# Softmax row sums inverted by GpSimd with a power of -1 in place of VectorE's reciprocal, in an attention block with an fp8 linear layer

## The chip, the cores and the metric

The kernel runs on one core of one Trainium2 chip. The metric is the device time of one execution in microseconds. Engine names in the rows: PE is TensorE, PEld its weight loads, DVE is VectorE, ACT is ScalarE, POOL is GpSimd, SP is SyncE, whose queue issues all the transfers.

## The reference, cut to what matters

The input x has the shape (8, 2048, 512). It is layer-normalised, then goes through an attention whose sequence axis is the first one (length n = 8), so that each of the 2048 columns is a batch entry with 16 heads of width 32, and through a linear layer with fp8 operands. The outputs and x are added.

```python
xn = _layernorm(x)
qkv = xn @ Wqkv.T + bqkv                    # n = 8, b = 2048, 16 heads of 32
mask = _prompt_mask(n, 4, 7, x.dtype)       # rows 0 to 3 see keys 0 to 3, rows 4 to 7 see all 8
scores = mask + scale * jnp.einsum('bnd,bmd->bnm', q, k)
attn = jax.nn.softmax(scores, axis=-1)      # the row sums of this softmax are what is inverted
out = jnp.einsum('bnm,bmd->bnd', attn, v)   # then @ Wproj.T + bproj
x = x + attention(xn) + fp8_linear(xn)
```

## The kernel before

The work is cut into 128 tiles of 128 rows (one sequence position, 128 batch entries). Eight consecutive tiles are the eight positions of the same 128 batch entries and make a group; there are 16 groups. Because of the mask, the first four tiles of a group see 4 keys ("light") and the last four see 8 ("heavy"). With so few keys, scores and the weighted sum of values are made by elementwise products and reductions and not by TensorE: one unit is 2048 products per partition. A light tile has one unit on each side, a heavy tile has two.

The kernel is one software pipeline. Every engine runs the same list of slots (`run_slots`), one slot for each tile, and does in slot j the stage with lag L for tile n = j - L. The lags that matter here: VectorE's statistics 1, the power that makes `rstd` 2, x's split into two fp16 parts 3, scores (L_QK) 8, exponential and row sum (L_SOFT) 9, probabilities and products with the values (L_PV) 11, the sum over these products (L_SUM) 12, its split 13, output projection and residual sum (L_PROJ) 15. Engines are in order and synchronise by counting semaphores: a wait holds everything that is behind it on the same engine. The order inside a slot is written by hand:

- VectorE: `bn_stats` (L722), `o_nat` sums of one or two units (L731), `bn_aggr` (L736), product and reduction of the first unit of scores (L694, L698), `row_sum` (L745), reciprocal (L748), the second unit of scores if there is one, row maximum (L758), its subtraction (L761).
- ScalarE: the exponential (L473) is first in the slot and waits for that subtraction; behind it lie, among others, both halves of the normalisation, the splits and `projected` (L516).
- GpSimd: `probs` (L399), the first unit of `prod_pv` (L388), the residual sum into `xs` (L407, waits for `projected`), the split of `o` (L412), `rstd` as a power of -0.5 on one column (L418), the split of `x` (L423), and, for a heavy tile, the second unit of `prod_pv` (L388).

`exps` and `inv_sum` have rings of four tiles, `probs` of two, `prod_pv` of four units. `row_sum` has one buffer. The slots overlap so that scores are heavy in four slots of eight and the products with the values in another four.

Of the kernel before, what the change touches and what calls it, by code (L numbers as in the profile page):

```python
# [5 lines left out]
F32 = mybir.dt.float32  # L6
# [4 lines left out]
ALU = mybir.AluOpType  # L11
ACT = mybir.ActivationFunctionType
AX_X = mybir.AxisListType.X

P = 128
# [3 lines left out]
H = 16  # L19
# [25 lines left out]
def keys_of(n):  # L45
    return PROMPT if n % N < PROMPT else N
# [17 lines left out]
def tile_count(i, n):  # L64
    return i * PAIR + (n + 1)
# [11 lines left out]
def after(eng, sem, count):  # L77
    if not isinstance(count, int) or count > 0:
        eng.wait_ge(sem, count)  # L79
# [20 lines left out]
def attention_and_fp8_linear(nc, x, Wqkv, bqkv, Wproj, bproj, Wffn, bffn, out):  # L100
# [3 lines left out]
    with ExitStack() as ctx:  # L104
        def sb(name, shape, dt):
            return ctx.enter_context(nc.sbuf_tensor(name, shape, dt))
# [25 lines left out]
        out_scale = sb("out_scale", [P, 1], F32)  # L132
        out_unscale = sb("out_unscale", [P, 1], F32)
        minus_half = sb("minus_half", [P, 1], F32)

        xn = sb("xn", [P, 4, C], F32)
# [18 lines left out]
        scores = sb("scores", [P, H, N], F32)  # L156
        shifted = sb("shifted", [P, H, N], F32)
        exps = sb("exps", [P, 4, H, N], F32)
        row_sum = sb("row_sum", [P, H], F32)
        inv_sum = sb("inv_sum", [P, 4, H], F32)  # L160
        probs = sb("probs", [P, 2, H, N], F32)
        prod_pv = sb("prod_pv", [P, PRODS, QUAD], F32)
        o_nat = sb("o_nat", [P, 2, C], F32)
# [32 lines left out]
        consts_set = sem("consts_set")  # L196
# [139 lines left out]
        @block.gpsimd  # L336
        def _(pool):
            nc.gpsimd.memset(ident[:, :], 0.0).then_inc(consts_set, 1)
            pool.wait_ge(consts_set, 1)
            nc.gpsimd.affine_select(out=ident[:, :], in_=ident[:, :], compare_op=ALU.not_equal, fill=1.0,  # L340
                                    base=0, pattern=[[-1, P]], channel_multiplier=1).then_inc(ident_ready, 1)
            nc.gpsimd.memset(ones[:, :], 1.0).then_inc(consts_set, 1)
            nc.gpsimd.memset(minus_half[:, :], -0.5).then_inc(consts_set, 1)
            nc.gpsimd.memset(out_bias_rows[:, :], 0.0).then_inc(consts_set, 1)

            pool.wait_ge(amax_parts, 1)
            nc.gpsimd.partition_all_reduce(amax[:, 6:8], amax[:, 4:6], P,
                                           bass.bass_isa.ReduceOp.max).then_inc(amax_ready, 1)

            def split_into_rows(b, rows):  # L350

                hi, mid, low = bias_parts
                nc.gpsimd.tensor_copy(hi, b).then_inc(bias_steps, 1)
                pool.wait_ge(bias_steps, 2)
                nc.gpsimd.tensor_tensor(bias_rest, b, hi, ALU.subtract).then_inc(bias_steps, 1)
                pool.wait_ge(bias_steps, 3)
                nc.gpsimd.tensor_copy(mid, bias_rest).then_inc(bias_steps, 1)
                pool.wait_ge(bias_steps, 4)
                nc.gpsimd.tensor_tensor(bias_rest, bias_rest, mid, ALU.subtract).then_inc(bias_steps, 1)
                pool.wait_ge(bias_steps, 5)  # L360
                nc.gpsimd.tensor_copy(low, bias_rest).then_inc(bias_steps, 1)
                pool.wait_ge(bias_steps, 6)
                pool.wait_ge(consts_set, 4)
                for k, part in enumerate((hi, mid, low)):
                    nc.gpsimd.tensor_copy(rows[32 * k:32 * k + 1, :], part[32 * k:32 * k + 1, :]).then_inc(bias_rows_ready, 1)
                    pool.wait_ge(bias_rows_ready, k + 1)

            pool.wait_ge(scales_ready, 1)
            pool.wait_ge(bk_loaded, 16)
            nc.gpsimd.tensor_scalar(k_bias[:, :], k_bias[:, :], scale[:, 0:1], 1.0, ALU.mult, ALU.mult).then_inc(k_bias_ready, 1)  # L370
            pool.wait_ge(bq_loaded, 16)
            nc.gpsimd.tensor_scalar(q_bias[:, :], q_bias[:, :], scale[:, 0:1], 1.0, ALU.mult, ALU.mult).then_inc(q_bias_ready, 1)
            pool.wait_ge(out_biases_loaded, 32)
            nc.gpsimd.tensor_tensor(bo_all, bo_all, bffn_all, ALU.add).then_inc(bias_steps, 1)
            pool.wait_ge(bias_steps, 1)
            nc.gpsimd.tensor_scalar(bo_all, bo_all, out_unscale[:, 0:1], 1.0, ALU.mult,
                                    ALU.mult).then_inc(out_biases_scaled, 1)

            def products(i, n, unit):
                u, h, heads = unit  # L380
                keys = keys_of(n)
                v = v_all[:, (n // N) % 2, h * D:(h + heads) * D, 0:keys].rearrange("p (h d) m -> p h d m", d=D)
                p = probs[:, n % 2, h:h + heads, 0:keys].unsqueeze(2).broadcast_to([P, heads, D, keys])
                o = prod_pv[:, u % PRODS, :].rearrange("p (h d m) -> p h d m", d=D, m=keys)
                after(pool, probs_ready, tile_count(i, n))
                after(pool, v_kept, tile_count(i, N * (n // N) + keys - 1))
                after(pool, pv_summed, unit_count(i, u - PRODS))
                nc.gpsimd.tensor_tensor(o, v, p, ALU.mult).then_inc(pv_multiplied, 1)  # L388

            def slot(i, j):  # L390
                if at(i, j, L_SOFT):
                    pool.wait_ge(out_bias_summed, 1)
                    split_into_rows(bo_all, out_bias_rows)
                if live(i, j, L_PV):
                    n = j - L_PV
                    keys = keys_of(n)
                    after(pool, inv_ready, tile_count(i, n))
                    after(pool, pv_multiplied, unit_count(i, last_unit(n - 2)))
                    nc.gpsimd.tensor_tensor(probs[:, n % 2, :, 0:keys], exps[:, n % 4, :, 0:keys],  # L399
                                            inv_sum[:, n % 4, :].unsqueeze(2).broadcast_to([P, H, keys]),  # L400
                                            ALU.mult).then_inc(probs_ready, 1)
                    products(i, n, head_units(n)[0])
                if live(i, j, L_PROJ):
                    n = j - L_PROJ
                    after(pool, proj_scaled, tile_count(i, n))
                    after(pool, res_loaded[n % 4], 16 * ring_count(i, n, 4))
                    nc.gpsimd.tensor_tensor(xs[:, n % 4, :], xs[:, n % 4, :], projected[:, :],  # L407
                                            ALU.add).then_inc(y_ready, 1)
                if live(i, j, L_SPLIT):
                    n = j - L_SPLIT  # L410
                    after(pool, o_hi_ready, tile_count(i, n))
                    nc.gpsimd.tensor_tensor(o16[:, n % 2, C:2 * C], o_nat[:, n % 2, :], o16[:, n % 2, 0:C],  # L412
                                            ALU.subtract).then_inc(o_lo_ready, 1)
                if live(i, j, L_CENTRE):
                    n = j - L_CENTRE
                    after(pool, var_ready, tile_count(i, n))
                    after(pool, xn_ready, tile_count(i, n - 2))
                    nc.gpsimd.tensor_tensor(rstd[:, n % 2, :], var_eps[:, :], minus_half[:, :],  # L418
                                            ALU.pow).then_inc(rstd_ready, 1)
                if live(i, j, L_NORM):  # L420
                    n = j - L_NORM
                    after(pool, x_hi_q_ready, tile_count(i, n))
                    nc.gpsimd.tensor_tensor(x16[:, n % 2, C:2 * C], xn[:, n % 4, :], x16[:, n % 2, 0:C],  # L423
                                            ALU.subtract).then_inc(x_lo_ready, 1)
                if live(i, j, L_PV):
                    n = j - L_PV
                    for unit in head_units(n)[1:]:
                        products(i, n, unit)

            run_slots(pool, slot)  # L430
# [206 lines left out]
        def _(dve):  # L637
# [64 lines left out]
            def slot(i, j):  # L702
# [37 lines left out]
                if live(i, j, L_SOFT):  # L740
                    n = j - L_SOFT
                    keys = keys_of(n)
                    after(dve, exps_ready, tile_count(i, n))
                    after(dve, inv_ready, tile_count(i, n - 1))
                    nc.vector.tensor_reduce(row_sum[:, :], exps[:, n % 4, :, 0:keys], AX_X, ALU.add).then_inc(sum_ready, 1)  # L745
                    after(dve, sum_ready, tile_count(i, n))
                    after(dve, probs_ready, tile_count(i, n - 4))
                    nc.vector.reciprocal(inv_sum[:, n % 4, :], row_sum[:, :]).then_inc(inv_ready, 1)  # L748
                if live(i, j, L_QK):
                    n = j - L_QK  # L750
                    keys = keys_of(n)
# [35 lines left out]
```

## Time and profile before

| | |
|---|---|
| median of 3 runs | 1708.37 us (1707.04 to 1708.56) |
| profiled execution, its own time | 1709.81 us |
| its span, first to last instruction | 1707.7 us |
| outside the span | 2.1 us |
| mean granted TensorE clock | 0.978 of full speed |
| busy shares | PE 89%, DVE 89%, POOL 80%, ACT 60% |

The span is that of one execution. Busy durations of neighbouring instructions of one engine overlap by some hundredths of a microsecond, so what an instruction takes from its engine is read from start to start rather than from its duration.

### The profile page before, as it was taken

How to read it: one execution, taken by the hardware profiler on the slowest of the kernel's cores; microseconds unless marked ns; L12 is line 12 of the kernel's file. 1: busy time of each engine (PE TensorE's matmuls, PEld its weight loads, DVE VectorE, ACT ScalarE, POOL GpSimd, SP SyncE). 2: the span in 40 equal slices, each digit the busy share in tenths (PEclk: the TensorE clock that was granted, in tenths of full speed). 3: DMA queues.
4: the chain of work that ended last, by engine and by line, in shares of the span. 5: the costliest groups of instructions: out<-in, count | busy, mean ns of one | idle time of the engine just before them, and what ended most of it. 6: DMA issues, size and time to landing. Idle time of an engine off the chain costs nothing.

```text
span 1707.7 us, 24850 instructions
## 1 busy us (share of the span) xinstructions
PE 1517.0 (89%) x6791; PEld 677.6 (40%) x6913; DVE 1518.7 (89%) x1380; ACT 1025.5 (60%) x1946; POOL 1373.5 (80%) x854
## 2 busy tenths in 40 slices
PE   4998898989989998998989899898998989899855
PEld 3443343434434443443434344343443434344312
DVE  6499898989989999999989899898998899999892
ACT  5665666656656666556566666666666666666422
POOL 2368879697896979879697887969788796978877
PEclk8999999999999999999999999999999999999978
DMA  5343534445354354444444444444444444453332
GB/s 188 72 99 90 123 99 109 117 99 130 98 124 105 97 130 98 117 112 111 109 105 113 106 116 105 114 111 101 119 105 119 105 105 116 104 124 85 90 71 77
DMA packets 366532, 184.30 MB, mean 108 GB/s; under 512 B 314160, under 2 KB 314160, under 8 KB 366384
## 3 DMA queue, kind: packets, MB, share of 16 engines
q1 hardware_dynamic: 366384, 182.53, 43.9%
q8 instruction: 68, 1.11, 0.3%
q14 instruction: 80, 0.66, 0.2%
HBM read 73.41 MB, written 33.55 MB: 63 GB/s over the span
## 4 chain that ended last, share of the span: by engine, by line
POOL 35%; issue 30%; DVE 26%; PE 4%; ACT 3%; POOLq 1%; DVEq 1%; DMA 0%; ACTq 0%; SPq 0%
POOL prod_pv L388 22%; DVE prod_qk L694 14%; DVE scores L698 6%; POOL o L412 4%; POOL x L423 4%; POOL xs L407 3%; POOL rstd L418 2%; DVE stats L722 2%; PE k_ps L579 1%; PE v_ps L579 1%; POOL probs L399 1%; DVE q_ps L758 1%; DVE row_sum L745 1%; PE q_ps L579 1%; POOLq L79 1%
## 5 line engine op out<-in xcount | busy, mean ns | idle before, releaser
L388 POOL TENSOR_TENSOR prod_pv<-kv,probs 128x2048 f32<-128x2048 f32 x192 | 813.0, 4234 | 16.2 <-POOL probs L399 11.1
L731 DVE TENSOR_REDUCE o_nat<-prod_pv 128x256 f32<-128x2048 f32 (+1 forms) x192 | 436.1, 2284 | 92.3 <-POOL prod_pv L388 72.5
L698 DVE TENSOR_REDUCE scores<-prod_qk 128x64 f32<-128x2048 f32 x192 | 439.4, 2288 | 7.3
L579 PE MATMUL k_ps<-wqkv_hi,xT 128*128 128x512 f16 x1024 | 334.1, 388 | 118.2 <-DMA xT<-x 118.1
L694 DVE TENSOR_TENSOR prod_qk<-q_ps,kv 128x2048 f32<-128x2048 f32 x192 | 432.0, 2250 | 2.5 <-ACT kv L534 2.5
L407 POOL TENSOR_TENSOR xs<-xs,projected 128x512 f32<-128x512 f32 x128 | 162.4, 1269 | 238.5 <-ACT projected L516 237.9
L579 PE MATMUL proj_ps<-wproj_hi,oT 128*128 128x512 f16 x1032 | 336.4, 388 | 6.3 <-ACT proj_ps L527 6.3
L579 PE MATMUL v_ps<-wqkv_hi,xT 128*128 128x512 f16 x1024 | 326.0, 380 | 0.0
L579 PE MATMUL q_ps<-wqkv_hi,xT 128*128 128x512 f16 x1024 | 325.4, 379 | 0.0
L473 ACT ACTIVATE exps<-shifted,exp_scale 128x64 f32<-128x64 f32 (+1 forms) x128 | 47.8, 373 | 365.8 <-DVE shifted L761 365.6
L579 PEld LDWEIGHTS k_ps<-wqkv_hi,xT 128*128 128x128 f16 x1024 | 101.8, 99 | 272.7 <-issue 144.8
L543 ACT ACTIVATE kv<-v_ps 128x512 f32<-128x512 f32 x128 | 141.3, 1104 | 113.9 <-PE v_ps L579 113.8
L579 PE MATMUL proj_ps<-wproj_lo,oT 128*128 128x512 f16 x516 | 201.1, 390 | 0.0
L579 PE MATMUL k_ps<-wqkv_lo,xT 128*128 128x512 f16 x512 | 198.9, 388 | 0.0
L579 PE MATMUL v_ps<-wqkv_lo,xT 128*128 128x512 f16 x512 | 194.5, 380 | 0.0
L579 PE MATMUL q_ps<-wqkv_lo,xT 128*128 128x512 f16 x512 | 194.0, 379 | 0.0
L423 POOL TENSOR_TENSOR x<-xn,x 128x512 f16<-128x512 f32 x128 | 148.3, 1159 | 17.4 <-ACT x L510 17.4
L534 ACT ACTIVATE kv<-k_ps 128x512 f32<-128x512 f32 x128 | 75.4, 589 | 133.1 <-PE k_ps L579 133.1
L412 POOL TENSOR_TENSOR o<-o_nat,o 128x512 f16<-128x512 f32 x128 | 148.3, 1159 | 5.6 <-ACT o L491 5.6
L579 PEld LDWEIGHTS proj_ps<-wproj_hi,oT 128*128 128x128 f16 x1032 | 102.7, 100 | 125.4 <-issue 9.8
L579 PEld LDWEIGHTS v_ps<-wqkv_hi,xT 128*128 128x128 f16 x1024 | 100.5, 98 | 121.8 <-issue 1.7
L579 PEld LDWEIGHTS q_ps<-wqkv_hi,xT 128*128 128x128 f16 x1024 | 100.2, 98 | 120.8
(115 smaller groups left out, 1727.9 us busy)
## 6 DMA issues: line engine op xcount, KB each, us to landing
xn<-in_L_attn_x SPq DMA_DIRECT2D x128, 256.0 KB, 2.8
xs<-in_L_attn_x SPq DMA_DIRECT2D x128, 256.0 KB, 2.9
out<-xs SPq DMA_DIRECT2D x128, 256.0 KB, 2.0
xT<-x SPq DMA_TRANSPOSE x256, 3.0
kv<-in_L_attn_Wqkv SPq DMA_DIRECT2D x3, 1024.0 KB, 10.6
oT<-o SPq DMA_TRANSPOSE x128, 3.2
kv<-in_L_ffn_weight SPq DMA_DIRECT2D x1, 1024.0 KB, 5.6
kv<-in_L_attn_Wproj SPq DMA_DIRECT2D x1, 1024.0 KB, 14.6
```

The costliest lines, as they stand in the source:

```text
L388: nc.gpsimd.tensor_tensor(o, v, p, ALU.mult).then_inc(pv_multiplied, 1)
L407: nc.gpsimd.tensor_tensor(xs[:, n % 4, :], xs[:, n % 4, :], projected[:, :], ALU.add).then_inc(y_ready, 1)
L412: nc.gpsimd.tensor_tensor(o16[:, n % 2, C:2 * C], o_nat[:, n % 2, :], o16[:, n % 2, 0:C], ALU.subtract).then_inc(o_lo_ready, 1)
L418: nc.gpsimd.tensor_tensor(rstd[:, n % 2, :], var_eps[:, :], minus_half[:, :], ALU.pow).then_inc(rstd_ready, 1)
L423: nc.gpsimd.tensor_tensor(x16[:, n % 2, C:2 * C], xn[:, n % 4, :], x16[:, n % 2, 0:C], ALU.subtract).then_inc(x_lo_ready, 1)
L473: nc.scalar.activation(exps[:, n % 4, :, 0:keys], shifted[:, :, 0:keys], ACT.Exp, scale=exp_scale[:, 0:1]).then_inc(exps_ready, 1)
L534: nc.scalar.activation(k_all[:, g % 2, n % N, :], k_ps[:, :], ACT.Copy).then_inc(k_kept, 1)
L543: nc.scalar.activation(v_all[:, g % 2, :, n % N], v_ps[:, :], ACT.Copy).then_inc(v_kept, 1)
L579: last = nc.tensor.matmul(acc[:, :], t[:, tc, :], w[:, c, col:col + 512], start=first and k == 0, stop=k == len(parts) - 1, skip_group_che ...
L694: nc.vector.tensor_tensor(prod_qk[:, :].rearrange("p (m c) -> p m c", c=C), qb, k, ALU.mult).then_inc(qk_multiplied, 1)
L698: nc.vector.tensor_reduce(scores[:, :, m0:m0 + 4].rearrange("p h m -> p m h"), prod_qk[:, :].rearrange("p (m h d) -> p m h d", h=H, d=D), ...
L731: nc.vector.tensor_reduce(o_nat[:, n % 2, h * D:(h + heads) * D], prod_pv[:, u % PRODS, :].rearrange("p (c m) -> p c m", m=keys), AX_X, AL ...
```

## The change

GpSimd makes the inverse of the row sums itself, with `pow` and an exponent of -1, in the same slot and directly in front of the probabilities that use it. VectorE's reciprocal is gone. So `row_sum` gets a ring of four tiles (it has to live from VectorE's slot n + 9 to GpSimd's slot n + 11), `inv_sum` gets one buffer, and the waits follow: VectorE waits for the probabilities of tile n - 4 ahead of the row sum and no longer for `inv_ready` and `sum_ready`; GpSimd waits for `sum_ready` of tile n and `probs_ready` of tile n - 1 ahead of the power, and for its own `inv_ready` ahead of the probabilities. A constant column of -1 is set once at the start.

```diff
+        minus_one = sb("minus_one", [P, 1], F32)
...
-        row_sum = sb("row_sum", [P, H], F32)
-        inv_sum = sb("inv_sum", [P, 4, H], F32)
+        row_sum = sb("row_sum", [P, 4, H], F32)
+        inv_sum = sb("inv_sum", [P, H], F32)
...
+            nc.gpsimd.memset(minus_one[:, :], -1.0).then_inc(consts_set, 1)
...
-                pool.wait_ge(consts_set, 4)
+                pool.wait_ge(consts_set, 5)
...
+                    after(pool, sum_ready, tile_count(i, n))
+                    after(pool, probs_ready, tile_count(i, n - 1))
+                    nc.gpsimd.tensor_tensor(inv_sum[:, :], row_sum[:, n % 4, :],
+                                            minus_one[:, :].broadcast_to([P, H]), ALU.pow).then_inc(inv_ready, 1)
                     after(pool, inv_ready, tile_count(i, n))
                     after(pool, pv_multiplied, unit_count(i, last_unit(n - 2)))
                     nc.gpsimd.tensor_tensor(probs[:, n % 2, :, 0:keys], exps[:, n % 4, :, 0:keys],
-                                            inv_sum[:, n % 4, :].unsqueeze(2).broadcast_to([P, H, keys]),
+                                            inv_sum[:, :].unsqueeze(2).broadcast_to([P, H, keys]),
                                             ALU.mult).then_inc(probs_ready, 1)
...
                     after(dve, exps_ready, tile_count(i, n))
-                    after(dve, inv_ready, tile_count(i, n - 1))
-                    nc.vector.tensor_reduce(row_sum[:, :], exps[:, n % 4, :, 0:keys], AX_X, ALU.add).then_inc(sum_ready, 1)
-                    after(dve, sum_ready, tile_count(i, n))
                     after(dve, probs_ready, tile_count(i, n - 4))
-                    nc.vector.reciprocal(inv_sum[:, n % 4, :], row_sum[:, :]).then_inc(inv_ready, 1)
+                    nc.vector.tensor_reduce(row_sum[:, n % 4, :], exps[:, n % 4, :, 0:keys], AX_X,
+                                            ALU.add).then_inc(sum_ready, 1)
```

## Rows read from the trace of the kernel before

**Rows 1.** The page: busy time by engine, and the chain that ended last.

```profile
PE 1517.0 (89%) x6791; PEld 677.6 (40%) x6913; DVE 1518.7 (89%) x1380; ACT 1025.5 (60%) x1946; POOL 1373.5 (80%) x854
...
POOL 35%; issue 30%; DVE 26%; PE 4%; ACT 3%; POOLq 1%; DVEq 1%; DMA 0%; ACTq 0%; SPq 0%
```

**Rows 2.** The chain in order of time: start, length, what; group starts, last group, drain.

```profile
143.63 4.47 POOL prod_pv L388
...
1454.52 4.48 POOL prod_pv L388
...
1568.56 4.49 POOL prod_pv L388
```

**Rows 3.** Busy time by stretch: one group, its GpSimd part, its VectorE part.

```profile
844.95:945.52 100.57, 91.66 (x417) 40.95 (x423) 93.21 (x85) 62.93 (x121) 85.10 (x52) 1.00 0.45 110
844.95:893.97 49.02, 41.80 (x189) 18.37 (x190) 42.42 (x41) 32.30 (x62) 48.62 (x27) 1.00 0.45 104
893.97:945.52 51.55, 49.86 (x228) 22.57 (x233) 50.79 (x45) 30.63 (x59) 36.48 (x26) 1.00 0.45 116
```

**Rows 4.** GpSimd's timeline: start, length, instruction, idle time before it.

```profile
853.41 0.41 POOL L399 TENSOR_TENSOR probs<-exps,inv_sum 128x128 f32<-128x128 f32 x1
853.90 4.54 POOL L388 TENSOR_TENSOR prod_pv<-kv,probs 128x2048 f32<-128x2048 f32 x1
...
866.85 0.42 POOL L399 TENSOR_TENSOR probs<-exps,inv_sum 128x128 f32<-128x128 f32 x1
867.43 4.54 POOL L388 TENSOR_TENSOR prod_pv<-kv,probs 128x2048 f32<-128x2048 f32 x1 [0.16 <-POOL probs L399]
...
880.38 0.42 POOL L399 TENSOR_TENSOR probs<-exps,inv_sum 128x128 f32<-128x128 f32 x1
...
889.42 4.51 POOL L388 TENSOR_TENSOR prod_pv<-kv,probs 128x2048 f32<-128x2048 f32 x1
```

**Rows 5.** VectorE's timeline in the same group.

```profile
893.97 2.29 DVE L731 TENSOR_REDUCE o_nat<-prod_pv 128x256 f32<-128x2048 f32 x1 [2.96 <-POOL prod_pv L388]
...
900.75 0.21 DVE L745 TENSOR_REDUCE row_sum<-exps 128x16 f32<-128x64 f32 x1
901.00 0.25 DVE L748 RECIPROCAL inv_sum<-row_sum 128x16 f32<-128x16 f32 x1
901.17 0.17 DVE L758 TENSOR_REDUCE q_ps<-scores 128x16 f32<-128x64 f32 x1
901.37 0.22 DVE L761 TENSOR_TENSOR shifted<-scores,q_ps 128x64 f32<-128x64 f32 x1
901.51 0.69 DVE L722 BATCH_NORM_STATS2 stats<-xn 128x6 f32<-128x512 f32 x1
...
935.48 0.25 DVE L748 RECIPROCAL inv_sum<-row_sum 128x16 f32<-128x16 f32 x1
```

**Rows 6.** The chain in order of time, from VectorE through ScalarE to GpSimd.

```profile
940.57 0.30 DVE shifted L761
...
944.79 0.58 ACT projected L516
```

**Rows 7.** GpSimd's groups of instructions within the same group of tiles, shapes apart.

```profile
L407 POOL TENSOR_TENSOR xs<-xs,projected 128x512 f32<-128x512 f32 x8 | 10.2, 1271 | 14.5 <-ACT projected L516 14.5
```

**Rows 8.** Groups of instructions over the whole span, shapes apart.

```profile
L418 POOL TENSOR_TENSOR rstd<-var_eps,minus_half 128x1 f32<-128x1 f32 x128 | 70.4, 550 | 27.4 <-ACT var_eps L482 27.3
L399 POOL TENSOR_TENSOR probs<-exps,inv_sum 128x128 f32<-128x128 f32 x64 | 26.1, 409 | 0.0
L399 POOL TENSOR_TENSOR probs<-exps,inv_sum 128x64 f32<-128x64 f32 x64 | 19.3, 302 | 0.0
```

**Rows 9.** The chain at the start of the pipeline and GpSimd's timeline in its drain.

```profile
106.62 0.31 POOL probs L399
114.97 0.31 POOL probs L399
126.99 0.40 POOL probs L399
...
1664.59 0.41 POOL L399 TENSOR_TENSOR probs<-exps,inv_sum 128x128 f32<-128x128 f32 x1
1676.35 0.40 POOL L399 TENSOR_TENSOR probs<-exps,inv_sum 128x128 f32<-128x128 f32 x1
```

## The prediction

> **What bounds the kernel now.** I read the page first. VectorE and TensorE are busy for 89% of the span and GpSimd for 80%, but the chain that ended last runs through GpSimd more than through VectorE (35% against 26%) and hardly through TensorE [rows 1]. So the shares do not tell which engine pays; the chain in order of time does. It repeats with the groups of eight tiles: from 143.63 to 1454.52 us lie 13 groups, 100.84 us each [rows 2]. I took one of them apart.
>
> The group from 844.95 to 945.52 us has two halves [rows 3]. In the first, 49.02 us long, GpSimd is busy for 48.62 us and sets the pace: the slots in which its heavy tiles fall. VectorE waits in it, the last time for 2.96 us in front of the `o_nat` sum at 893.97 [rows 5], until GpSimd's product, begun at 889.42, is done [rows 4]. In the second half, 51.55 us, VectorE is busy for 50.79 us and does not wait again, and GpSimd is busy for 36.48 us. The way back is the subtraction of the maximum at 940.57 (VectorE), the exponential and what lies behind it on ScalarE's queue up to `projected`, ending at 945.37 [rows 6], and the residual sum on GpSimd, which waits for it and begins the next group's first half. Over the group GpSimd idles for 14.5 us, all in front of that sum [rows 7]. The reader should see that GpSimd's idle fifth lies wholly in the half where VectorE is the bound, and VectorE's in the half where GpSimd is. Work moved from one to the other in every slot is paid in one half and earned in the other.
>
> **The change part by part.**
>
> Removed: 128 reciprocals on VectorE. From start to start, row sum and reciprocal take 901.17 - 900.75 = 0.42 us in a light slot. What comes behind the row sum no longer depends on it, so the row sum alone should hold the engine for its duration less the usual overlap; the subtraction of 0.22 us is followed after 0.14 us [rows 5], an overlap of 0.08. So 0.21 - 0.08 = 0.13 us stay and 0.29 us are saved per slot. It counts only where VectorE is the bound. Between 893.97 and 940.57 four reciprocals lie on the path, from the one at 901.00 to the one at 935.48 [rows 5]. In the other slots of the group VectorE waits for GpSimd anyway and the saving only lengthens that wait. Over the run: 13 intervals between first halves with four, one with five (it is a slot longer: 1454.52 to 1568.56 is 114.0 us [rows 2]) and the one before the drain with about five, 62 in all, so 62 x 0.29 = 18.0 us earned. The waits that VectorE loses (`inv_ready`, `sum_ready`) and the one that moves ahead of the row sum cost nothing: the probabilities of tile n - 4 are two slots old by then, over 16 us even where slots are shortest, and VectorE cannot run that far ahead of GpSimd because its `o_nat` sum waits for GpSimd's products of the slot before.
>
> Added on GpSimd, in each slot: one power over 16 columns and one wait of GpSimd for itself. The row sum it reads is two slots old, and the probabilities of tile n - 1 are its own of the slot before, so neither of these waits is late. The wait for itself is like the one that already stands between the probabilities and their product: 853.41 to 853.90 for a duration of 0.41, and 866.85 to 867.43 for 0.42 [rows 4], so 0.08 to 0.16 us of drain, 0.12 taken. Behind it on the queue is everything that GpSimd has. Three of a group's powers fall in the first half, in front of the probabilities at 853.41, 866.85 and 880.38 [rows 4]; the other five fall where GpSimd has the 14.5 us of idle time as cover [rows 7]. First halves: 15 of them, the last starting at 1568.56 [rows 2], give 45 powers; the probabilities at 106.62, 114.97 and 126.99 are on the chain at the start and those at 1664.59 and 1676.35 hold the drain [rows 9], so 50 in all. With x for the power's duration the change in time is 50 (x + 0.12) - 18.0 us.
>
> The price of x is the open term. The trace has a power on one column, 0.550 us, and multiplications on 64 and 128 columns at 0.302 and 0.409 us [rows 8]. The two multiplications give 0.0017 us a column and 0.195 us fixed, so the first column of a power costs some 0.354 us above an ordinary instruction. Lower end: all of that is paid once and each further column costs what a multiplied one does, 0.550 + 15 x 0.0017 = 0.575 us. Upper end: each column costs as much as the first, 0.195 + 16 x 0.354 = 5.86 us. The nearest row is the one-column power, 15 columns away, and it leans to neither end. I take a further column at a tenth of the first one's excess, 0.035 us: a column of multiplication costs a hundredth of that instruction's fixed part, so latency is paid once in this engine's loops, but a power is many operations and not one. That gives x = 0.550 + 15 x 0.035 = 1.08 us. The sum: 50 x 1.20 - 18.0 = 60.0 - 18.0 = +42 us. The profiled execution (1707.7 us of span and 2.1 around it) is 1.4 us above the median of the runs, and I add to the median: 1708.4 + 42 = 1750.
>
> One rule speaks against the change. The measured rows put the reciprocal at 0.29 us of VectorE and the one-column power alone at 0.55 us of GpSimd. The Trainium skill, page "GPSIMD Engine Reference", section "When to use GPSIMD", assigns elementwise work to VectorE and calls GpSimd about twice as slow for two inputs; by a factor of two on the reciprocal's 0.25 us the power would be 0.5 us and the change 50 x 0.62 - 18 = +13 us, which the one-column row already contradicts from above. The same page, section "Performance pitfalls for Q7 kernels", says that dependent fp32 operations take four cycles each and independent ones overlap, and section "Performance versus the Vector engine" that long bodies run at about three operations per cycle. 
>
> Other queues: later splits of `x` and `o` delay SyncE's transfers by the same microsecond per slot in the first half, where TensorE has 49.02 - 41.80 us free [rows 3], so nothing waits for that. The added constant is one small memset at the start, hidden behind the weight loads.
>
> **The rivals.**
>
> *Power without overlap across columns.* x from 3.3 to 5.86 us. Then GpSimd is the bound in every slot. Its group without idle time is 100.57 - 14.5 = 86.1 us, and eight powers make it 86.1 + 8 (x + 0.12). This overtakes the half-and-half sum, 100.84 - 1.16 + 3 (x + 0.12), from x = 2.6 us on. At x = 5.86 a group is 133.9 us, +33.1 us in 16 groups, 2238 us; at 3.3 it is 113.5 us, 1910 us. For it: GpSimd's mathematics is software and the excess of 0.354 us for one column is large. Against it: the other loops of this engine pay latency once.
>
> *A power in between*, x from 1.6 to 3.3 us: 50 x 1.72 - 18 = +68 us, 1776, up to 1910 us.
>
> *VectorE is the bound throughout* (the other side). If GpSimd's share of 80% were real cover in all slots, the power would be free and all 128 reciprocals earned: 128 x 0.29 = 37 us, 1671 us. Against it: 48.62 of 49.02 us busy and VectorE's wait of 2.96 us at the end of the half. Within the sum above the sign turns at 50 (x + 0.12) = 18.0, x = 0.24 us, less than half of the power on one column.
>
> *No measurable change*: x near 0.25 to 0.3 us, which the one-column row excludes too unless durations of the power overstate what it takes; then the drain of the queue would have to be cheaper than shown.
>
> **How the numbers follow.** What a measurement of this kernel can tell from no change is about 0.2%, 3.4 us. My forecast is the cheap power, x from 0.575 to 1.6 us: 60%; its own range is 50 x 0.695 - 18 = +17 us to +68 us, 1725 to 1776 us. The power in between gets 18%, the one without overlap 18%, no change 2%, VectorE throughout 2%. The range reaches from just below the forecast's lower end, 1722, over the in-between case to 1910 us and leaves out the other three, 22% less what of them lies at the border. Both ends of the power's price stay named: 1725 and 2238 us. Slower 96%, same 2%, faster 2%.
>
> **What the profile after would show.** A new GpSimd line with a power of 16 columns in front of each `probs`: its duration is x, and I read it from start to start as well. VectorE's row sum followed after 0.13 to 0.2 us. The first half of a group, from the residual sum to the end of the last product of the heavy tiles, longer by 3 (x + 0.12), about 3.6 us; the second shorter by 1.16 us; GpSimd's idle time per group in front of the residual sum down from 14.5 us to some 7 to 8 us. If that idle time is gone, the power is dearer than 2.6 us and the first rival's sum holds. I am wrong if the first half grows by less than three powers, which would mean that GpSimd had cover there, or if a group grows although x is small, which would point to a wait that I took as never late (the row sum's, or the self-wait's drain).

## The result and the profile after

The changed kernel takes 1867.1 us (median of 4 runs, 1866.1 to 1868.3) against 1708.5 us of the kernel before: a ratio of 1.0929, 95% interval 1.0910 to 1.0948, or 159 us more. The forecast of 1750 us had the direction right and the size wrong; the range, 1722 to 1910 us, holds the time, because it took in the case that the prediction called a power in between and gave 18%; the case that it forecast with 60% ended at 1776 us.

The page of the changed kernel: busy time by engine and the chain that ended last, then two groups of instructions (busy, mean ns of one, idle time before them).

```profile
PE 1580.7 (85%) x6791; PEld 694.4 (37%) x6913; DVE 1498.2 (80%) x1252; ACT 1026.4 (55%) x1946; POOL 1742.4 (93%) x983
...
POOL 71%; issue 22%; PE 4%; POOLq 1%; DMA 1%; SPq 0%; ACT 0%; DVE 0%; ACTq 0%
...
L401 POOL TENSOR_TENSOR inv_sum<-row_sum,minus_one 128x16 f32<-128x16 f32 x128 | 372.5, 2910 | 0.0
...
L413 POOL TENSOR_TENSOR xs<-xs,projected 128x512 f32<-128x512 f32 x128 | 162.4, 1269 | 18.6 <-ACT projected L522 17.7
```

Four readings. The power takes 2.91 us, not 1.08. VectorE has left the chain altogether, which it held with 26% before [rows 1]. GpSimd's idle time in front of the residual sum, 14.5 us in one group before [rows 7], is 18.6 us in the whole run, where it was 238.5 before:

```profile
L407 POOL TENSOR_TENSOR xs<-xs,projected 128x512 f32<-128x512 f32 x128 | 162.4, 1269 | 238.5 <-ACT projected L516 237.9
```

And GpSimd's busy time grew by 369 us, while the kernel grew by 159: more than half of the added work went where GpSimd had been idle.

One group of eight tiles, busy time by engine (PE, PEld, DVE, ACT, POOL, then the granted clock), to be read against the first of [rows 3]:

```profile
810.81:921.52 110.71, 96.84 (x417) 42.25 (x424) 91.85 (x77) 63.17 (x120) 108.17 (x61) 0.95 0.41 101
```

GpSimd is busy for 108.17 of 110.71 us; 2.3 of the 2.5 us left are its waits for itself (13 of them), seen in its timeline (start, length, instruction, idle time before it):

```profile
844.03 4.49 POOL L390 TENSOR_TENSOR prod_pv<-kv,probs 128x2048 f32<-128x2048 f32 x1
848.49 2.90 POOL L401 TENSOR_TENSOR inv_sum<-row_sum,minus_one 128x16 f32<-128x16 f32 x1
851.54 0.41 POOL L405 TENSOR_TENSOR probs<-exps,inv_sum 128x128 f32<-128x128 f32 x1 [0.16 <-POOL inv_sum L401]
852.11 4.53 POOL L390 TENSOR_TENSOR prod_pv<-kv,probs 128x2048 f32<-128x2048 f32 x1 [0.16 <-POOL probs L405]
856.60 1.27 POOL L413 TENSOR_TENSOR xs<-xs,projected 128x512 f32<-128x512 f32 x1
```

From start to start the power with its wait takes 851.54 - 848.49 = 3.05 us of the queue, 3.06 on the mean of all 128. There is no half of the group left in which VectorE sets the pace. The prediction's sum for that case, 86.1 us and eight times the power, gives 86.1 + 8 x 3.06 = 110.6 us; 110.71 were measured, in this group and on the mean of 13 (from the probabilities at 203.01 us to those at 1642.37).

VectorE's timeline in the changed kernel, around the place where the reciprocal stood:

```profile
855.34 0.21 DVE L751 TENSOR_REDUCE row_sum<-exps 128x16 f32<-128x64 f32 x1
855.47 0.22 DVE L762 TENSOR_REDUCE q_ps<-scores 128x16 f32<-128x64 f32 x1
855.73 0.22 DVE L765 TENSOR_TENSOR shifted<-scores,q_ps 128x64 f32<-128x64 f32 x1
855.86 0.69 DVE L728 BATCH_NORM_STATS2 stats<-xn 128x6 f32<-128x512 f32 x1
...
907.35 0.28 DVE L751 TENSOR_REDUCE row_sum<-exps 128x16 f32<-128x128 f32 x1
907.57 2.29 DVE L700 TENSOR_TENSOR prod_qk<-q_ps,kv 128x2048 f32<-128x2048 f32 x1
```

The row sum is indeed followed after 0.13 us. But the row maximum behind it now takes 0.22 us instead of 0.17 and is followed later: from the row sum to the statistics it is 0.52 us against 0.76 before [rows 5], 0.24 us saved and not 0.29. Where the second unit of scores follows, the next start is 0.22 us away and that product is 2.29 us long, longer than its like behind a reciprocal (shown with e3 below).

### The profile page after: what moved, and what is told of

It is laid out like the page before. It is cut to its first block, busy times and chain, and to the rows that moved or that the text cites. A ratio compares the mean times of both kernels' runs of the same rounds, so it can differ in the third digit from the quotient of the medians.

```text
span 1866.5 us, 24844 instructions
## 1 busy us (share of the span) xinstructions
PE 1580.7 (85%) x6791; PEld 694.4 (37%) x6913; DVE 1498.2 (80%) x1252; ACT 1026.4 (55%) x1946; POOL 1742.4 (93%) x983
## 4 chain that ended last, share of the span: by engine, by line
POOL 71%; issue 22%; PE 4%; POOLq 1%; DMA 1%; SPq 0%; ACT 0%; DVE 0%; ACTq 0%
POOL prod_pv L390 25%; POOL inv_sum L401 19%; POOL o L418 8%; POOL xs L413 7%; POOL x L429 7%; POOL rstd L424 3%; POOL probs L405 2%; PE k_ps L585 2%; PE v_ps L585 1%; POOLq L79 1%; DMA xT<-x 1%; PE q_ps L585 1%; SPq L325 0%; SPq L317 0%; ACT kv L549 0%
## 5 line engine op out<-in xcount | busy, mean ns | idle before, releaser
L585 PE MATMUL k_ps<-wqkv_hi,xT 128*128 128x512 f16 x1024 | 378.1, 434 | 202.5 <-DMA xT<-x 202.3
L401 POOL TENSOR_TENSOR inv_sum<-row_sum,minus_one 128x16 f32<-128x16 f32 x128 | 372.5, 2910 | 0.0
L585 PEld LDWEIGHTS k_ps<-wqkv_hi,xT 128*128 128x128 f16 x1024 | 111.5, 109 | 383.0 <-issue 249.5
L585 PE MATMUL k_ps<-wqkv_lo,xT 128*128 128x512 f16 x512 | 226.9, 443 | 0.0
L413 POOL TENSOR_TENSOR xs<-xs,projected 128x512 f32<-128x512 f32 x128 | 162.4, 1269 | 18.6 <-ACT projected L522 17.7
```

The costliest lines, as they stand in the source:

```text
L401: nc.gpsimd.tensor_tensor(inv_sum[:, :], row_sum[:, n % 4, :], minus_one[:, :].broadcast_to([P, H]), ALU.pow).then_inc(inv_ready, 1)
L585: last = nc.tensor.matmul(acc[:, :], t[:, tc, :], w[:, c, col:col + 512], start=first and k == 0, stop=k == len(parts) - 1, skip_group_che ...
```

## The experiments

### What a power costs

A probe at GpSimd's start, before anything depends on it: powers and multiplications of several widths.

```diff
+            for name, width in PROBES:
+                nc.gpsimd.tensor_tensor(probe_out[:, col:col + width], probe_a[:, 0:width],
+                                        probe_b[:, 0:1].broadcast_to([P, width]), getattr(ALU, name))
+                col += width
```

> The kernel before with a probe in GpSimd's start-up: powers on 1, 2, 4, 8, 16, 32 and 64 columns (base 3.0, exponent -1 broadcast), multiplications on 1 and 16 columns, and three more powers on 16 columns: exponent as a full operand, base 1.0, exponent -0.5. Theory L (a further column has a fixed price of its own, paid without overlap between columns): the two points known, 0.55 us for 1 column (before) and 2.91 us for 16 (after), give 0.157 us a column, so 0.71, 1.02, 1.65, 2.91, 5.42 and 10.5 us for 2 to 64 columns, and the three variants at 16 columns all at 2.9 us. Rival S (columns are worked in chunks, so that the price goes in steps): 1 to 4 columns at 0.55 us and then jumps. Rival V (the price depends on the numbers or on the broadcast: the one-column power has a base near 1 and an exponent of -0.5): the variants come out far from 2.9 us, and one of them near 0.6 us. Multiplications at 0.20 and 0.22 us in any case.

The groups of the probe, shapes apart. L361 has the exponent as a full operand, L363 a base of 1.0, L365 an exponent of -0.5.

```profile
L358 POOL TENSOR_TENSOR prod_pv<-prod_pv 128x64 f32<-128x64 f32 x1 | 10.5, 10515 | 0.0
L358 POOL TENSOR_TENSOR prod_pv<-prod_pv 128x32 f32<-128x32 f32 x1 | 5.4, 5408 | 0.0
...
L361 POOL TENSOR_TENSOR prod_pv<-prod_pv 128x16 f32<-128x16 f32 x1 | 2.9, 2897 | 0.0
L365 POOL TENSOR_TENSOR prod_pv<-prod_pv 128x16 f32<-128x16 f32 x1 | 2.9, 2888 | 0.0
L363 POOL TENSOR_TENSOR prod_pv<-prod_pv 128x16 f32<-128x16 f32 x1 | 2.9, 2887 | 0.0
L358 POOL TENSOR_TENSOR prod_pv<-prod_pv 128x8 f32<-128x8 f32 x1 | 2.6, 2591 | 0.0
L358 POOL TENSOR_TENSOR prod_pv<-prod_pv 128x4 f32<-128x4 f32 x1 | 1.0, 1012 | 0.0
...
L358 POOL TENSOR_TENSOR prod_pv<-prod_pv 128x2 f32<-128x2 f32 x1 | 0.7, 707 | 0.0
```

2, 4, 32 and 64 columns lie on one line: (10.515 - 0.707) / 62 = 0.158 us a column over about 0.39 us fixed, and the power on one column of the kernel before, 0.55 us, lies on it too. On 16 columns the bases 3.0 and 1.0, the exponents -1 and -0.5, and an exponent broadcast or in full give the same time. There are no steps at these widths. The 8 columns at 2.59 us and a power on 16 columns at 3.70 us did not fit, so the probe was run again in another order.

> The probe again in another order, powers on 1, 16, 8, 16, 8, 16, 8, 12, 24, 16 and 8 columns and three more on 16. In the first probe 8 columns took 2.59 us and 16 columns 3.70 us, 0.94 and 0.79 us above the line through the others (0.405 + 0.157 per column), while three later powers on 16 columns took 2.89 us. Theory (those two were held up once by something outside of them, whatever the width): 8 columns at 1.66 us, 12 at 2.29, 24 at 4.2 and 16 at 2.9 us in nearly every place, and an excess, if any, again some 5 to 10 us into the span and on whatever stands there. Rival (8 columns have a slow path of their own): 2.59 us each time.

Powers on 8 and 12 columns from that run:

```profile
L358 POOL TENSOR_TENSOR prod_pv<-prod_pv 128x8 f32<-128x8 f32 x1 | 1.6, 1632 | 0.0
...
L358 POOL TENSOR_TENSOR prod_pv<-prod_pv 128x12 f32<-128x12 f32 x1 | 2.3, 2264 | 0.0
```

In the second probe 8 columns take 1.63 us in three of four places, 12 take 2.26, 24 take 4.15 and 16 take 2.89 to 2.93. The excess is back on whatever stands some 6 to 12 us into the span: 2.60 us for one 8 and 3.71 us for one 16. It goes with the place in time and not with the width; what it is was not looked for. The line is settled: 0.39 us and 0.158 us for each column.

### Does VectorE's saving count at all

The kernel before with its reciprocal, and the power added beside it.

```diff
                     after(pool, inv_ready, tile_count(i, n))
+                    after(pool, pow_done, tile_count(i, n - 1))
+                    nc.gpsimd.tensor_tensor(unused[:, 0:16], inv_sum[:, n % 4, 0:16],
+                                            minus_one[:, :].broadcast_to([P, 16]), ALU.pow).then_inc(pow_done, 1)
+                    after(pool, pow_done, tile_count(i, n))
```

> The kernel before, with VectorE's reciprocal kept, and the same power on 16 columns added on GpSimd in front of the probabilities; its result is not used. Theory (GpSimd is the bound in every slot of the changed kernel, so the removed reciprocals earned nothing): a group is 86.1 + 8 x 3.03 = 110.3 us here too, and the time is that of the changed kernel, 1867 us, within 4 us. Rival (the savings on VectorE still count in part): slower than the changed kernel by the 18 us of the prediction's term, 1885 us.

1875.1 us, a ratio of 1.0975 (1.0953 to 1.0997), 8 us above the changed kernel: between the theory's 1867 and the rival's 1885. A group is 111.0 us (924.44 to 1035.47 us in the chain in order of time); on the mean of 13 groups it is 111.1 against 110.7 us in the changed kernel, 0.4 us more, which is 6 to 7 of the 8 us. VectorE is back on the chain, with 9.2% for its products and 4.9% for its score reductions, where the changed kernel shows 0% for all of it. So GpSimd is the bound but not far ahead of VectorE: taking the reciprocals away under the power is worth some 8 us, where run e3 below earns 13 without any inverse.

### The change with a cheap instruction, and with none

In the place of the power a multiplication (its result is minus the row sum, so probabilities are not normalised):

```diff
-                                            minus_one[:, :].broadcast_to([P, H]), ALU.pow).then_inc(inv_ready, 1)
+                                            minus_one[:, :].broadcast_to([P, H]), ALU.mult).then_inc(inv_ready, 1)
```

> The changed kernel with a multiplication on the same 16 columns in the place of the power (probabilities are scaled by minus the row sum: this changes the computation). Theory (two halves, three instructions of GpSimd in the bound half, four reciprocals saved in the other): x = 0.22 us, 50 x (0.22 + 0.12) - 18 = -1 us, 1707.5 us. Rival (VectorE is the bound everywhere and GpSimd's work is under cover): -37 us, 1671 us. Rival (each instruction of GpSimd counts in each slot): 128 x 0.34 - 18 = +26 us, 1734 us.

And without power and wait, so that the row sum multiplies where its inverse should:

```diff
-                    after(pool, probs_ready, tile_count(i, n - 1))
-                    nc.gpsimd.tensor_tensor(inv_sum[:, :], row_sum[:, n % 4, :],
-                                            minus_one[:, :].broadcast_to([P, H]), ALU.pow).then_inc(inv_ready, 1)
-                    after(pool, inv_ready, tile_count(i, n))
...
-                                            inv_sum[:, :].unsqueeze(2).broadcast_to([P, H, keys]),
+                                            row_sum[:, n % 4, :].unsqueeze(2).broadcast_to([P, H, keys]),
```

> The changed kernel without the power and without its wait: the probabilities are scaled with the row sum itself (this leaves out the inverse). It shows what the removal from VectorE is worth alone. Theory: 62 reciprocals on the path at 0.29 us, -18 us, 1690 us, with the interval from group to group shorter by 1.16 us. Rival (all 128 count): -37 us, 1671 us. Rival (they are hidden): 1708 us.

1695.3 us without any inverse, a ratio of 0.9919 (0.9903 to 0.9936): 13 us, where 62 reciprocals at 0.29 us were to give 18. Divided by 62 it is 0.21 us each. A group takes 99.9 us instead of 100.8 (means of 13). VectorE's timeline in that kernel, beside the 0.41 us from row sum to product at 909.02 in the kernel before:

```profile
902.62 0.21 DVE L747 TENSOR_REDUCE row_sum<-exps 128x16 f32<-128x64 f32 x1
902.84 2.29 DVE L696 TENSOR_TENSOR prod_qk<-q_ps,kv 128x2048 f32<-128x2048 f32 x1
905.16 2.29 DVE L700 TENSOR_REDUCE scores<-prod_qk 128x64 f32<-128x2048 f32 x1
```

From the row sum to the reduction of scores it is 2.54 us here. The same three in the kernel before, with the reciprocal between them:

```profile
909.02 0.21 DVE L745 TENSOR_REDUCE row_sum<-exps 128x16 f32<-128x64 f32 x1
909.26 0.25 DVE L748 RECIPROCAL inv_sum<-row_sum 128x16 f32<-128x16 f32 x1
909.43 2.23 DVE L694 TENSOR_TENSOR prod_qk<-q_ps,kv 128x2048 f32<-128x2048 f32 x1
911.70 2.29 DVE L698 TENSOR_REDUCE scores<-prod_qk 128x64 f32<-128x2048 f32 x1
```

2.68 us there, so 0.14 us saved in this place, behind the row sum of a light tile. Over all slots of the two traces without a wait in them (150 to 1580 us) the means are 0.15 us in such places, 0.21 behind the row sum of a heavy tile and 0.26 where the maximum follows. The four places on the path of a group are one, two and one of these, 0.83 us together and 0.21 each, which is what the run gives. The neighbour had been shorter behind a reciprocal than behind a row sum, and that part is given back.

With the multiplication it is 1712.4 us, a ratio of 1.0024 (1.0014 to 1.0034). The theory on record said 1707.5 us; it missed by 5 us, which is the part by which the reciprocals are worth less than 18 us. The multiplication with its wait costs 1712.4 - 1695.3 = 17 us. It takes 0.22 us, and 0.37 from start to start, so these are some 46 places, near the 50 that were counted. Even with a multiplication on the same 16 columns in the place of the power the change would have been a small loss.

### Fewer columns

e1's edit with 8 columns of 16.

> The kernel before, reciprocals kept, with a power on 8 of the 16 columns added in front of the probabilities, result unused. It takes GpSimd 1.66 us and 0.16 for the wait, 1.8 us a slot. Theory (two halves): 3 powers a group count as long as 86.1 + 8 y is below 100.84 + 3 y, which it is (100.5 against 106.2), so 50 x 1.8 = +90 us, 1798 us. Rival (GpSimd's idle fifth covers them all, 14.5 us a group against 8 x 1.8 = 14.4): 1709 us. Rival (each one counts): +230 us, 1939 us.

1795.6 us, 1.0509 (1.0488 to 1.0530): +87 us against +90 expected, and a group takes 106.1 us on the mean of 13, where the theory had 106.2. GpSimd's added work per group, 8 x 1.8 = 14.4 us, would fit under its 14.5 us of idle time to the tenth, and still three eighths of it are paid in full. This is the clearest single run for the two halves.

### The same number of powers in two places

Half of the tiles by power, half by reciprocal. `by_power(n)` is true for the light tiles, n % 8 < 4, in e5, for the heavy ones in e6, and for 0 < n % 8 < 4 in e7.

```diff
+                    if by_power(n):
                         after(pool, sum_ready, tile_count(i, n))
...
+                    if not by_power(n):
+                        after(dve, sum_ready, tile_count(i, n))
+                        nc.vector.reciprocal(inv_sum[:, n % 4, :], row_sum[:, n % 4, :]).then_inc(inv_ready, 1)
```

> The changed kernel with the power for light tiles alone; heavy tiles keep VectorE's reciprocal. Half of the powers, all of them in the half of a group where VectorE is the bound and GpSimd idles for 14.5 us. Theory (place decides, not number): 4 x 3.07 = 12.3 us a group fit under the idle time, two powers at the start of the pipeline cost 6 us, and two reciprocals a group less on VectorE's path earn some 0.19 us each by run e3, 6 us: 1708 us, within 4 us of before. Rival (the cost goes by the number of powers): half of +159 us, 1788 us.

> The mirror image: the power for heavy tiles alone, light tiles keep the reciprocal. As many powers as in e5, but three of four stand in the half that GpSimd bounds. Theory: 48 of them on the path x 3.07 = +147 us, less some 6 us for two reciprocals a group, 1849 us, although GpSimd has idle time left. Rival (number of powers): 1788 us.

Light tiles 1729.6 us, 1.0125 (1.0108 to 1.0142); heavy tiles 1846.3 us, 1.0806 (1.0785 to 1.0828). As many powers, 64, cost 21 us in one place and 138 in the other, so it is the place that decides. e6 came within 3 us of the sum. e5 missed by 21 us, and the trace says by what. GpSimd's timeline in e5:

```profile
904.09 2.91 POOL L414 TENSOR_TENSOR inv_sum<-row_sum,minus_one 128x16 f32<-128x16 f32 x1
...
912.44 1.16 POOL L433 TENSOR_TENSOR o<-o_nat,o 128x512 f16<-128x512 f32 x1
```

And VectorE's:

```profile
913.73 2.29 DVE L752 TENSOR_REDUCE o_nat<-prod_pv 128x512 f32<-128x2048 f32 x1 [1.57 <-POOL o L433]
```

`o_nat` is a ring of two, so the sum of tile n waits for the split of tile n - 2 (line 730 of the kernel before), and that split stands on GpSimd's queue behind the first light tile's power. Before, it ended at 900.28 us and the sum began at 902.23: 1.95 us of slack for 3.07 us of power, which leaves the 1.1 us by which a group is longer (101.9 us against 100.8). That I had not counted; I had looked at whether the products come in time and they do.

One step further: the first light tile goes back to VectorE.

> As e5 (power for light tiles alone), but the first light tile of each group is inverted by VectorE again. In e5 a group took 1.1 us more than before, and VectorE waited 1.57 us in front of the first light sum for GpSimd's split of o, which stands in the queue behind that tile's power; before, the split ended 1.95 us ahead of that sum (900.28 and 902.23 us), less than the 3.07 us of a power. Theory (that wait is the whole loss): three powers a group stay, all under the idle time, the 1.1 us a group go away and 0.4 us of VectorE's path stay saved; two powers at the start cost 6 us: 1708 us, within 4 us. Rival (powers cost in proportion, also where GpSimd idles): three quarters of e5's loss, 1724 us.

1703.1 us, 0.9965 (0.9952 to 0.9978): the loss is gone, and the kernel is 0.35% faster than before while GpSimd computes 48 powers of 2.91 us. A group takes 100.3 us, 0.5 less than before, near the 0.4 expected. The whole is 5 us faster where I expected no change, because the powers on the chain at the start did not cost their 6 us. In the chain in order of time the heavy products at the start are begun at 128.33 us against 127.47 in the kernel before:

```profile
99.85 2.87 POOL inv_sum L414
...
108.45 2.87 POOL inv_sum L414
...
118.17 2.87 POOL inv_sum L414
...
128.33 4.55 POOL prod_pv L402
```

Three powers of nearly 3 us are on the chain and the tile behind them is 0.9 us later, as late as the very first probabilities already are (92.04 against 91.08 us), which have no power in front of them. GpSimd's timeline of the kernel before shows what held those slots:

```profile
111.59 1.16 POOL L412 TENSOR_TENSOR o<-o_nat,o 128x512 f16<-128x512 f32 x1 [0.95 <-ACT o L491]
...
123.61 1.16 POOL L412 TENSOR_TENSOR o<-o_nat,o 128x512 f16<-128x512 f32 x1 [4.62 <-ACT o L491]
```

GpSimd waited for ScalarE there, and in e7 it does not. So of the three powers at the start that the prediction counted among its 50, the two that e7 has (those at 108.45 and 118.17 us) were covered. In the changed kernel, with all three in place, the product that begins at 143.59 us in the kernel before begins at 145.70, 2.1 us later and not 9.

### The reciprocal moved within VectorE's order

If much of the reciprocal's price was the time between the row sum and the reciprocal that depends on it, another place on VectorE should do as well as another engine.

```diff
                     nc.vector.tensor_reduce(row_sum[:, :], exps[:, n % 4, :, 0:keys], AX_X, ALU.add).then_inc(sum_ready, 1)
-                    after(dve, sum_ready, tile_count(i, n))
-                    after(dve, probs_ready, tile_count(i, n - 4))
-                    nc.vector.reciprocal(inv_sum[:, n % 4, :], row_sum[:, :]).then_inc(inv_ready, 1)
...
                     nc.vector.tensor_reduce(row_max, scores[:, :, 0:keys], AX_X, ALU.max).then_inc(max_ready, 1)
+                if live(i, j, L_SOFT):
+                    n = j - L_SOFT
+                    after(dve, sum_ready, tile_count(i, n))
+                    after(dve, probs_ready, tile_count(i, n - 4))
+                    nc.vector.reciprocal(inv_sum[:, n % 4, :], row_sum[:, :]).then_inc(inv_ready, 1)
...
                     after(dve, max_ready, tile_count(i, n))
```

> The kernel before, with VectorE's reciprocal kept and moved in VectorE's own order from right behind the row sum to between the row maximum and its subtraction. It fills the latency between those two and no longer waits for the row sum. Theory (much of what removing the reciprocal earned, 13 us in e3, was latency between dependent instructions, not work): 0.15 us a slot on the path for 62 slots, 9 us less, 1699 us. Rival (it is work): no change, 1708 us.

1695.4 us, 0.9924 (0.9910 to 0.9937): 13 us less than before, where the theory had 9, and as fast as e3, which has no inverse at all. VectorE's timeline in e8:

```profile
868.18 0.21 DVE L745 TENSOR_REDUCE row_sum<-exps 128x16 f32<-128x64 f32 x1
868.31 0.22 DVE L755 TENSOR_REDUCE q_ps<-scores 128x16 f32<-128x64 f32 x1
868.44 0.24 DVE L760 RECIPROCAL inv_sum<-row_sum 128x16 f32<-128x16 f32 x1
868.60 0.19 DVE L766 TENSOR_TENSOR shifted<-scores,q_ps 128x64 f32<-128x64 f32 x1
868.70 0.69 DVE L722 BATCH_NORM_STATS2 stats<-xn 128x6 f32<-128x512 f32 x1
```

From row sum to statistics 0.52 us with the reciprocal among them, as much as without it in the changed kernel. The reciprocal lies in the time between the maximum and the subtraction that depends on it, and the row sum is two instructions old when it is read.

> As e8, and one reciprocal of 32 columns for two tiles in every second slot. Theory: half of what is left of the reciprocal goes as well, 2 to 4 us under e8, 1696 us, close to e3's 1695 us without any inverse. Rival (nothing is left of it after e8): equal to e8. Rival (the second tile's probabilities now wait): slower than e8.

The last variant has `row_sum` in a ring of four, and every second slot one reciprocal over the 32 sums of two tiles:

```diff
-                if live(i, j, L_SOFT):
+                if live(i, j, L_SOFT) and (j - L_SOFT) % 2:
...
-                    nc.vector.reciprocal(inv_sum[:, n % 4, :], row_sum[:, :]).then_inc(inv_ready, 1)
+                    nc.vector.reciprocal(inv_sum[:, a:a + 2, :], row_sum[:, a:a + 2, :]).then_inc(inv_ready, 1)
```

1707.2 us, 0.9990 (0.9981 to 0.9999), 12 us worse than e8. Its waits show a new one (us in total, times, longest):

```profile
POOL probs L403 <- DVE inv_sum L765: 141.6, 32, 8.1
```

The older tile of a pair gets its inverse a slot late, at the end of VectorE's slot, when GpSimd already wants it; in each group it is two of the four pairs whose older tile waits. The last rival on record for this run holds in that it is slower than e8, though the tile that waits is the older one and not the second. Most of the 141.6 us stand in the place of idle time that GpSimd had anyway: in front of the residual sum it is 95.8 us here and 224.1 in e8.

## Why the prediction was right or wrong

**What bounds the kernel.** Right. A group has two halves, and of eight instructions added to GpSimd three are paid in one half and five have cover in the other: e4 (+87 against +90 us, a group of 106.1 against 106.2), e6 (1846 against 1849) and the price of the multiplication in e2 (17 us, 0.37 in some 46 places) follow the sum.

**The price of the power.** Wrong, and this is the step that failed: "I take a further column at a tenth of the first one's excess, 0.035 us". It is 0.158 us, so x = 2.91 us instead of 1.08. The reason given for it, that latency is paid once in this engine's loops, was read off multiplications and does not carry over: widths from 1 to 64 columns lie on one line, and each further column costs 45% of the first one's excess where a tenth was taken. Whether columns follow one another or overlap at that rate, a straight line cannot tell. The upper end was not right either: of the first column's 0.354 us only 0.158 belong to the column and the other 0.2 us are paid once. A single width of one operation cannot tell fixed from proportional, and I had only one. The measured x lies in the case of a power in between, not in the forecast one.

**Which sum applies.** The rival's sum with its turning point at x = 2.6 us was right, and so was the sign for it: GpSimd's idle time in front of the residual sum is gone. With 2.91 us and the wait of 0.12 it gives 86.1 + 8 x 3.03 = 110.3 us a group and 1708.4 + 16 x 9.5 = 1860 us, 7 us under the time; with the 3.06 us measured from start to start it is 9.7 us a group and 1864 us. The forecast's own sum with the same x gives 1708.4 + 50 x 3.03 - 18 = 1842 us, so 92 of the 117 us by which 1750 was missed are the price alone. The Trainium skill, page "GPSIMD Engine Reference", section "Performance pitfalls for Q7 kernels", says that a dependent chain of fp32 operations costs four cycles a step and that independent ones overlap. The prediction drew it into an estimate of 0.030 us a column; the probe measured 0.158, and the measurement decides. It does not show which part of the estimate fails, the overlap or the number of operations. That page's section "When to use GPSIMD", elementwise work to VectorE, holds here by far more than its factor of two for two inputs: 2.91 us against 0.25.

**The removed reciprocals.** Direction right, size off: 0.21 us each instead of 0.29 (e3), because the row sum is followed later than after 0.13 us where a product stands behind it (0.22), and because the instructions behind a row sum take longer than behind a reciprocal. Under the power, where GpSimd is the bound, the removal is worth 8 us and not 13 (e1 against the changed kernel); the sum that applies counted nothing for it.

**The wait for itself.** 0.16 us idle in front of most probabilities, 0.08 to 0.16 forecast.

**Waits taken as never late.** The row sum's is never late in the changed kernel. But one that stood already, VectorE's sum for the split of `o`, has 1.95 us of slack and a dear power uses it up (e5, removed in e7). It was missing from the argument. In the changed kernel VectorE waits for that split for 121.7 us in all, against 10.1 before, but it decides nothing there, since GpSimd has no idle time left; for a power placed under cover it does.

**TensorE.** Its mean granted clock in the group is 0.95 against 1.00 before: for about a tenth of the group it has the lower of its two levels (1.2 and 2.4 GHz). It was busy for 96.84 of 110.71 us (87%), against 91.66 of 100.57 (91%) before. This is not where the time went: GpSimd's gaps are 2.5 us in that group, and 2.3 of them are its waits for itself.

Where the 159 us lie, by GpSimd's probabilities in the two traces: the first ones begin at 94.80 instead of 91.08 us, 3.7 us later; the 15 intervals to those of the last group (at 1751.84 and 1599.33) take 148.8 us more, 9.9 each; and what follows is 6.3 us longer. So the two ends together make the sixteenth group that the sum counts. Open are the 3 us between 1864 and 1867. They lie mostly in the first two intervals, longer by 10.6 and 11.5 us instead of 9.7; why was not looked for.

## What to carry to other kernels

Before an operation moves to an engine whose price for it is known at one width only, measure a second width; most of the miss here is that slope. Where two engines take turns in setting the pace, idle time is cover only in the half where it lies and only as far as the nearest wait of the other engine allows: 64 powers cost 138 us or 21, and 48 in the right slots cost nothing. And look at an instruction's own neighbours before moving it to another engine: three lines further down on VectorE, the reciprocal filled a gap between two dependent instructions and gave all that its removal could give, 0.76%.

## What the runs showed of the hardware that I had not expected

- GpSimd's power costs 0.39 us and 0.158 us for each column of 128 partitions, from 1 to 64 columns, and on 16 columns the same for the bases 3.0 and 1.0, the exponents -1 and -0.5, broadcast or not; a multiplication on 16 columns takes 0.21 us. Sixteen reciprocals are 0.25 us on VectorE.
- On VectorE a short reduction and the same product of 2048 elements took 0.17 and 2.23 us behind a reciprocal (means of 57 and 56 in the kernel before) and 0.22 and 2.29 us behind a row sum (57 and 56 in e3). What the removal of an instruction saves depends on what then follows what.
- Some 5 to 12 us into the span two of GpSimd's powers took 0.8 to 1.0 us longer than their like, at about the same time in both probes and at different widths.
